# One fused cross-attention block: attention in batches of four half-width units, and a one-pass, tile-wise start

## The reference

```python
def _layernorm(x): return (x - mean(x)) / sqrt(var(x) + 1e-5)

def xattn(latents, context):          # latents = _layernorm(x)
    lat = layer_norm(latents, ln_lat_g, ln_lat_b)      # a second norm, then gain and bias
    ctx = layer_norm(context, ln_ctx_g, ln_ctx_b)
    q = heads(lat @ Wq); k, v = split(ctx @ Wkv); k = apply_rope(heads(k), cos, sin)
    attn = softmax(clip(q @ k.T * 64**-0.5, -11, 11))
    return concat(attn @ v) @ Wo + bo

x = x + tanh(g_xattn) * xattn(_layernorm(x), ctx)
x = x + tanh(g_ffn) * int8_matmul(_layernorm(x), rhs)  # both sides quantised, row and column scales
```

## Time and profile before

| What | us |
|---|---|
| median of three runs | 1541.34 |
| profiled execution, its own time | 1544.19 |
| its span (first to last instruction) | 1542.4 |
| TensorE (PE) busy | 1490.7 (97%) |
| VectorE (DVE) busy | 1287.8 (83%) |
| ScalarE (ACT) busy | 714.5 (46%) |
| GpSimd (POOL) busy | 127.8 (8%) |
| value products, L874 | 496.6 |
| score products, L861 | 426.4 |
| exps, L932 | 496.3 |
| adds, L1016 | 516.0 |
| clips, L1022 | 314.0 |

### The profile page before, as it was taken

How to read it: one execution, slowest core, us unless ns; L and a number is a source line. 1 busy time by engine, 2 the same in 40 slices (tenths; PEclk the granted TensorE clock), 3 DMA queues, 4 the chain that set the end, 5 groups by cost and what they waited for, 6 DMA issues and landing times. The chain is left out here.

```text
span 1542.4 us, 22114 instructions
## 1 busy us (share of the span) xinstructions
PE 1490.7 (97%) x7896; PEld 869.5 (56%) x7896; DVE 1287.8 (83%) x1256; ACT 714.5 (46%) x794; POOL 127.8 (8%) x72
## 2 busy tenths in 40 slices
PE   3999999999999899999999999999999999999997
PEld 3788888888886334444444444444444444444774
DVE  6866666676654999899899899899899899998887
ACT  3433222222223555555555555555555555555342
POOL 2220000000000210000000000000000000000765
PEclk9999999999999999999999999999999999999998
DMA  5665655546567540541440440441441442311652
GB/s 185 232 240 190 190 164 181 161 153 200 163 181 256 142 123 29 124 115 38 123 123 28 123 123 27 123 123 38 113 123 46 105 123 55 97 42 35 185 163 82
DMA packets 121998, 195.30 MB, mean 127 GB/s; under 512 B 18368, under 2 KB 67520, under 8 KB 115808
## 3 DMA queue, kind: packets, MB, share of 16 engines
q1 hardware_dynamic: 119360, 190.49, 42.5%
q10 hardware_dynamic: 2592, 4.20, 0.7%
HBM read 114.70 MB, written 79.95 MB: 126 GB/s over the span
## 5 line engine op out<-in xcount | busy, mean ns | idle before, releaser
L932 ACT ACTIVATE prob<-score_ps 128x1024 f32<-128x1024 f32 x512 | 496.3, 1022 | 377.7 <-PE score_ps L861 377.5
L1016 DVE TENSOR_TENSOR prob_sum<-prob_sum,prob 128x2048 f32<-128x2048 f32 x224 | 516.0, 2304 | 0.5
L874 PE MATMUL value_ps<-prob,v_st 128*64 128x512 f32 x2048 | 496.6, 606 | 10.6 <-DVE prob L1022 10.3
L861 PE MATMUL score_ps<-q_st,k_st 64*128 64x512 f32 x3072 | 426.4, 409 | 2.5 <-PEq L102 2.1
L861 PEld LDWEIGHTS score_ps<-q_st,k_st 64*128 64x128 f32 x3072 | 269.2, 185 | 256.4 <-ACT prob L932 187.8
L1022 DVE TENSOR_SCALAR prob<-prob 128x2048 f32<-128x2048 f32 x256 | 314.0, 1226 | 68.1 <-ACT prob L932 64.2
L874 PEld LDWEIGHTS value_ps<-prob,v_st 128*64 128x64 f32 x2048 | 124.2, 136 | 250.1 <-issue 201.7
L645 DVE TENSOR_TENSOR k_cos<-k_raw,rope 128x1024 f32<-128x1024 f32 x32 | 39.2, 1225 | 99.9 <-ACT k_raw L546 99.9
L551 ACT ACTIVATE v_out<-proj_ps 128x1024 f32<-128x1024 f32 x31 | 31.9, 1030 | 136.7 <-PE proj_ps L228 136.7
L546 ACT ACTIVATE k_raw<-proj_ps 128x1024 f32<-128x1024 f32 x31 | 31.9, 1029 | 105.2 <-PE proj_ps L228 104.0
L1331 POOL MEMSET unround<- 128x1 f32 x1 | 0.1, 98 | 872.6 <-POOLq L115 872.6
(11 more groups left out here) (119 smaller groups left out, 1306.2 us busy)
## 6 DMA issues: line engine op xcount, KB each, us to landing
k_st<-k_scr SPq DMA_DIRECT2D x128, 256.0 KB, 6.2
k_scr<-k_hi SPq DMA_DIRECT2D x64, 256.0 KB, 2.7
v_scr<-v_out SPq DMA_DIRECT2D x32, 512.0 KB, 3.5
k_scr<-k_lo SPq DMA_DIRECT2D x64, 256.0 KB, 4.0
q_st<-q_scr SPq DMA_DIRECT2D x16, 1024.0 KB, 10.5
v_st<-v_scr SPq DMA_DIRECT2D x16, 1024.0 KB, 13.3
q_scr<-q_hi SPq DMA_DIRECT2D x32, 256.0 KB, 3.3
q_scr<-q_lo SPq DMA_DIRECT2D x32, 256.0 KB, 3.4
```

What stands on the lines that cost most here:

```text
L861: last = pe.matmul(score_ps[:, half, a, :], k_st[slot][rows, k_part, s * P:(s + 1) * P], q_st[slot][rows, q_part, cols], start=(t == 0), s ...
L874: last = pe.matmul(value_ps[rows, cols], v_st[slot][:, s, rows], prob[:, s % PSLOT, a, cols], start=(s == 0), stop=(s == STEPS - 1))
L932: act.activation(prob[:, s % PSLOT, :, cols], score_ps[:, half, :, :], ACT.Exp, scale=SCALE).then_inc(exped, 1)
L1016: dve.tensor_tensor(total, total, prob[:, s % PSLOT, :, :], ALU.add).then_inc(added, 1)
```

## The change

It has two parts.

**Attention.** The queries of a pair are taken by halves: all 16 key steps for the first 512 queries, then for the others. A unit is one key step of one half (128x1024 with both heads), four units are a batch (BATCH_UNITS), a pair has 32 units in 8 batches, four a half. TensorE does the scores of a batch, 24 products, then the values of the batch before, 16. ScalarE makes four exps of the same size as before, VectorE one clip of 128x4096 and two adds of 128x2048 (one in the first batch of a half). Prob has two slots of one batch. The scores have three slots in PSUM, values and sums one bank each. Sums, reciprocals, the scaling and the stores are done by halves; a sum has 32 columns a head and partial sum, and VectorE joins the two partial sums in `reciprocals`. In `exps` the wait for the scores now stands last, behind those for the slot. SyncE loads pair n+2 after the reciprocals of half 0. The work on the feed-forward weight moves into pair 0 on VectorE, and the pieces of Wo to batches 1, 3, 4 and 5.

**Start.** The two norms of x become one pass with another constant under the root (eps_sq, factor 1 + eps). Chunk 0 is loaded, measured, scaled and transposed tile by tile. Wq is split by halves of its columns, and VectorE makes its rest. TensorE does 56 transposes of the identity before, and 10 behind, the transposes of chunk 0 (`keep_busy`). Tanh of the gates and its table load move behind context chunk 6.

```diff
-        def exps(n, s):
-            for half in range(2):
-                g = STEPS * n + s
-                act.wait_ge(scored, 2 * g + half + 1)
-                if not (first(n) and s < PSLOT):
-                    act.wait_ge(valued, g - PSLOT + 1)
-                    act.wait_ge(added, (STEPS - 1) * n + behind)
-                act.activation(prob[:, s % PSLOT, :, cols], score_ps[:, half, :, :], ACT.Exp, scale=SCALE)
+        def exps(n, b):
+            for u in range(b * BATCH_UNITS, (b + 1) * BATCH_UNITS):
+                if u % BATCH_UNITS == 0 and not (first(n) and b < 2):
+                    act.wait_ge(valued, BATCHES * n + b - 1)
+                    act.wait_ge(added, ADDS * (2 * n + (b - 2) // HALF_BATCHES) + 2 * ((b - 2) % HALF_BATCHES) + 1)
+                act.wait_ge(scored, UNITS * n + u + 1)
+                act.activation(prob[:, b % 2, u % BATCH_UNITS, :], score_ps[:, u % BANKS, :, :], ACT.Exp, scale=SCALE)
...
+        def scores(n, slot, b):
+            for u in range(b * BATCH_UNITS, (b + 1) * BATCH_UNITS):
+                if u >= BANKS:
+                    pe.wait_ge(exped, UNITS * n + u - BANKS + 1)
...
+        def sums(n, half):
+            for j in range(2):
+                for a in range(2):
+                    row = (2 * j + a) * SUM_ROWS
+                    last = pe.matmul(sum_ps[row:row + SUM_ROWS, :], ones[:, 0:SUM_ROWS], prob_sum[:, half, j, a, :],
+                                     start=True, stop=True)
+            for b in range(BATCHES):
+                scores(n, slot, b)
+                if b >= 1:
+                    values(n, slot, b - 1)
+                elif not first(n):
+                    values(n - 1, 1 - slot, BATCHES - 1)
+                if b == 1 and not first(n):
+                    sums(n - 1, 1)
+                if b == HALF_BATCHES + 1:
+                    sums(n, 0)
...
+            for b in range(BATCHES):
+                clip(n, b)
+                add_probs(n, b)
+                if b == 7 and not (isinstance(n, int) and n == ALLPAIRS - 1):
+                    ends.reciprocals(dve, n, 0)
+                if b == 1 and not first(n):
+                    ends.normalise(dve, n - 1, 0)
+                if b == 3 and not first(n):
+                    ends.reciprocals(dve, n - 1, 1)
+                if b == 5 and not first(n):
+                    ends.normalise(dve, n - 1, 1)
...
+        def after(n, where, before, loading=None):
+            ends.store_sums(sp, n, 0)
+            ends.load_sums(sp, n, 0)
+            if before is not None:
+                ends.store_output(sp, n - 1, 1, *before)
+            ends.store_reciprocals(sp, n, 0)
+            ends.load_reciprocals(sp, n, 0)
+            if loading is not None:
+                load(n + 2, *loading)
+            ends.store_sums(sp, n, 1)
+            ends.load_sums(sp, n, 1)
+            ends.store_output(sp, n, 0, *where)
+            ends.store_reciprocals(sp, n, 1)
+            ends.load_reciprocals(sp, n, 1)
...
+        def keep_busy(times):
+            for i in range(times):
+                pe.transpose(proj_ps[:, 3, 0:P], ident[:, :], ident[:, :])
+        pe.wait_ge(ident_set, 2)
+        keep_busy(WARM_EARLY)
+        turn_singles()
+        keep_busy(WARM_LATE)
...
+        for i, part in enumerate(SINGLE):
+            measure(0, 0, part)
+            if i:
+                normalise(0, 0, SINGLE[i - 1])
+        normalise(0, 0, SINGLE[-1])
+        wq_rest(0)
+        tok_split(0, 0)
+        wq_rest(1)
+        measure(1, 1)
```

More of the change, by code:

```diff
@@ L172, in load_reciprocals @@
+    def load_reciprocals(self, sp, n, half):
         late = self.late
-        sp.wait_ge(late.rec_stored, 16 * (n + 1))
+        sp.wait_ge(late.rec_stored[half], 16 * (n + 1))
         for a in range(2):
[L176 to L181, removed]
@@ L319, in banks, with turns_before @@
         return acc[:, first_bank:first_bank + 2, :]
-    def last_pass(n):
-        return 2 * n + 1 if isinstance(n, int) and n < QCH else n + QCH
-    def passes(n):
-        return (2 * n, 2 * n + 1) if n < QCH else (n + QCH,)
+    def turns_before(n, part):
+        return part[0].start if part is not CHUNK else n - 1
     def slot_read(eng, n):
@@ L830, in _ @@
         for n in range(2):
[L831 to L833 removed]
+            after(n, (0, n), (0, n - 1) if n else None, (n, 0, n + 2))
         with sp.Fori(1, ALLPAIRS // 2 - 1) as i:
@@ L836, in _ @@
                 n = 2 * i + slot
-                load(n + 2, slot, sp.snap((n + 2) // PAIRS), sp.snap((n + 2) % PAIRS))
-                ends.fetch_reciprocals(sp, n)
-                ends.store_output(sp, n, sp.snap(n // PAIRS), sp.snap(n % PAIRS))
-        sp.wait_ge(late.o_stored, 16 * (ALLPAIRS - 2))
+                here, last, ahead = [(sp.snap((n + d) // PAIRS), sp.snap((n + d) % PAIRS)) for d in (0, -1, 2)]
+                after(n, here, last, (slot,) + ahead)
+        n = ALLPAIRS - 2
+        after(n, (BATCH - 1, PAIRS - 2), (BATCH - 1, PAIRS - 3))
+        for half in range(2):
+            sp.wait_ge(late.o_stored[half], 16 * PAIRS)
         for t in range(2):
@@ new lines, in copy_values, with copy_sums @@
+        def copy_values(n, half):
+            act.wait_ge(valued, BATCHES * n + HALF_BATCHES * (half + 1))
+            if not first(n):
+                act.wait_ge(late.o_made, 2 * n + half - 1)
+            act.activation(late.o_raw[:, half * CH:(half + 1) * CH], value_ps[:, :], ACT.Copy).then_inc(late.o_copied, 1)
+        def copy_sums(n, half):
+            act.wait_ge(summed, 2 * n + half + 1)
+            if not (first(n) and half == 0):
+                act.wait_ge(late.sum_stored, 16 * (2 * n + half))
@@ new lines, in add_probs @@
+        def add_probs(n, b):
+            half, part = divmod(b, HALF_BATCHES)
+            total = prob_sum[:, half, :, :, :].rearrange("p j a c -> p j (a c)")
+            halves = [prob[:, b % 2, j:j + 2, :] for j in (0, 2)]
+            before = ADDS * (2 * n + half) + 2 * part - 1
+            dve.wait_ge(clipped, BATCHES * n + b + 1)
+            if part == 0:
+                if not first(n):
+                    dve.wait_ge(summed, 2 * (n - 1) + half + 1)
+                dve.tensor_tensor(total, halves[0], halves[1], ALU.add).then_inc(added, 1)
+                return
+            for j in range(2):
+                dve.wait_ge(added, before + j)
+                dve.tensor_tensor(total, total, halves[j], ALU.add).then_inc(added, 1)
@@ L1293, in turn @@
             if isinstance(t, int) and t == 3:
-                ends.reciprocals(dve, LAST)
+                for half in range(2):
+                    ends.reciprocals(dve, LAST, half)
             ending = isinstance(t, int) and t == TILES + 1
```

434 lines of the change are left out of this document (204 added, 230 removed).

## The result

Six runs of the changed kernel have a median of 1488.93 us (1487.94 to 1490.43), six of the kernel before on the same chip 1541.96 (1540.34 to 1545.64). The ratio is 0.9654, with an interval of 0.9641 to 0.9666: 53.0 us less, where 54 were predicted (1487). The profiled execution took 1488.88, its span 1486.9. That is 55.5 less span than before; the difference to 53.0 is mostly that the profiled execution of before lay 2.2 above its median and this one did not.

The account below looks back on a forecast made before the run. TensorE was taken to bound the attention, VectorE close behind. Attention 42.2 - 5.1 - 0.6 + 0.5 = 37.0 less, start and projections 17.0 less: 1490.2 from the profiled 1544.2, 1487 us against the median; range 1480 to 1507.

Parts of the forecast that it names:

- The switches: Attention: changes between score and value shapes lose 0.33 us a step; batching saves 42.2 us over 128 batches.
- Rival 4: Attention: the loss sits in each visit's waits or data, not shape, so batching saves nothing: 1529 us; chance 0.02.
- The sums: Sum products: four 32-column products at a time, 0.86 us a half plus 0.16 for a further switch, 5.1 more in all.
- rival 3: Sum products: only two run at a time, giving 1515 us; chance 0.09.
- VectorE: Attention: VectorE needs 26.4 us a half against TensorE's 27.4; clip 2.30, slack 2.4, slip up to 1.2; TensorE stays bound.
- rival 2: Attention: VectorE becomes the bound through gaps its present idling hides, 5 to 35 us more, likeliest 1500; chance 0.14.
- Pair 0: First attention pair: 61 us, with ScalarE's waits for Wo pieces passed on to TensorE; 0.6 more than now.
- The rhs work on VectorE, all in pair 0 now, uses those stalls: First attention pair: VectorE's rhs work fits into the stalls of about 1.7 + 3.3 + 3.5 + 1.3 us before exps.
- The order of the waits: ScalarE's exps: waiting for scores last spares at most two checks before each exp, keeping slack; costed at nothing.
- The last pair: End of attention: waits of 1.1 and 0.8 us, together the same as now; half-width last sum copy gives 0.5 back.
- The start: Start and projections: first product at 16.6, gain 11.3 us; clock 1.4 and chunk 2's stall 4.3; 17.0 less.
- rival 1: Start: dummy transposes don't lift the clock and push the first product to 20, giving 1492 us; chance 0.14.

Follow-up runs that it names:

- run 2: Changed kernel, but TensorE goes twice per batch from scores to values, two units each: 1566.90 us, ratio 1.0156 to the kernel before.
- run 3: Changed kernel, but exps wait for their scores first and then for the free slot: 1500.19 us, ratio 0.9728 to the kernel before.
- after: The changed kernel itself, with new attention and new start, against the kernel before: 1488.93 us, ratio 0.9654.
- run 4: Changed kernel, but sums use 64 columns a head, gathered in PSUM, without VectorE's join: 1510.85 us, ratio 0.9796 to the kernel before.
- run 8: Changed kernel with ScalarE's splits of Wo in batches 2, 4, 6, 7 of pair 0: 1490.79 us, ratio 0.9668 to the kernel before.
- run 10: Changed kernel with exps waiting for scores first in the pairs written out, last in the loop: 1486.98 us, ratio 0.9644 to the kernel before.
- run 12: Changed kernel with the edits of run 10 and run 11 and 34 dummy transposes for 10: 1483.68 us, ratio 0.9624 to the kernel before.
- run 9: Changed kernel, but GpSimd makes the rest of Wq again: 1495.28 us, ratio 0.9706 to the kernel before.
- run 11: Changed kernel with Wo's rest made by VectorE in place of GpSimd, last two pieces later: 1486.56 us, ratio 0.9644 to the kernel before.
- run 6: Changed kernel with 34 dummy transposes for 10 behind those of chunk 0: 1487.85 us, ratio 0.9647 to the kernel before.
- run 5: Changed kernel without its 66 dummy transposes: 1489.30 us, ratio 0.9659 to the kernel before.

## Why the prediction was right, point by point

**The switches.** Right in size, and shown: a round trip costs 0.35 (run 2) where I had worked out 0.33 from spacings in the earlier trace rows, and the waits inside a group cost nothing as long as they are met. Rival 4 is out. "So the shape" goes further than the runs: in run 3 the 0.11 that I had put down to entering the score shape is paid at unit 3 too, after a stop inside the group (0.33 to the next products for 0.22). A good part of the price therefore goes with a stop of the products, and no run separates shape, number format and stop for what is left.

**The sums.** Right: 1.00 a half against 1.02. Four at a time was my assumption; the starts in after and run 4, its opposite, show it, and rival 3 is out. The Trainium skill's statement on this (TensorEngine Tiling (Array Packing), Tiling Modes), that 128x32 tiles work as four independent ones, agrees with the 1.00; it gives no price for the change of mode, the 0.33 to 0.35 of the runs is one.

**VectorE.** Right in size: clips 2.286 (2.30), 95% busy, a slack over the clip of 2.1 in the batch shown and 1.0 at the least, where I had 2.4 less up to 1.2 of slipping. TensorE waits 4.3 us for clips in all, and rival 2 did not come in the steady part. Pair 0 is VectorE's, but it was so before the change: from 492.5 to 556.5 VectorE's only idle time was 12.7 us in front of clips, 9.0 of it one wait.

**Pair 0.** I predicted 61 for pair 0, and it was 60.87, but for an incomplete reason: "ACT stalls about 1.7 + 3.3 + 3.5 + 1.3 in front of exps, each passed on to TensorE". ScalarE's stalls were larger (15.5 in all), and when run 8 took them away pairs 0 and 1 together did not get shorter. The step that failed is "The rhs work on VectorE, all in pair 0 now, uses those stalls": it did not fit, and the backlog went into pair 1. Over a steady pair, pairs 0 and 1 lie 6.3 + 5.5 = 11.8, against 6.9 + 3.2 = 10.1 before: 1.7 more, where I had 0.6. Of the 1.7, 0.9 is idle time of TensorE (12.1 in the two pairs, 11.2 before) and 0.6 the later exps of pair 1, which is written out (8 x 0.08; run 10 gives 0.5 of it back). GpSimd's four pieces are part of the 11.8: where one runs, two adds take 6.67 in place of 4.62. They ran in the kernel before too, whose adds in pair 0 took 2.64 on average. That 61 was hit is luck: the cause I named was not the one that set the length.

**The order of the waits.** "I cost it at nothing" was wrong as a price. Against the batching with scores first it is worth 11.3 us: a pair of the loop takes 54.57 in place of 55.65, 13.0 in twelve pairs, and the pairs written out give 1.6 of it back. The batching has made the exps' start the tight link: that slack was 0.1 to 0.2, and the later exp used all of it. It did not harm the sum, since I took the exps' lag of 1.01 from the kernel before, and scores last gives just that (1.02). The pairs written out run at 1.09 and lose 0.08 a batch (6.65), which I had not foreseen. The mechanism is in the rows of run 3: the exp is late by 0.07 to 0.1 for each sequencer instruction that still has to run once the scores are there, none, one or two. Runs 10 and 12 bear it out, with none between and 1.00 to 1.02 in the loop and in the steady pair 14 alike. Why the compiled program places them in opposite ways in the loop and outside it stays open.

**The last pair.** The waits came as 0.71 for the clip and 1.00 for the add, where I had 1.1 and 0.8, in this chain of TensorE's timeline, answering to the earlier trace rows:

```profile
1362.08 3.65 PE L893 MATMUL value_ps<-prob,v_st 128*64 128x512 f32 x16 [0.71 <-DVE prob L1043]
1366.73 1.06 PE L907 MATMUL sum_ps<-prob_sum,ones 128*32 128x512 f32 x8 [1.00 <-DVE prob_sum L1059]
```

**The start.** First product at 16.30 (16.6), for the reason given: weights and affine on ScalarE, then the casts. Run 9 shows that taking GpSimd off VectorE's neighbourhood is 6.5 of the 11.6. The stall of chunk 2 is gone. The clock came as predicted, full for the transposes and half for 3.4 us from 16.8, behind the idle time before 16.30; run 11 shows that this fall need not come. So transposes do lift the clock, at 10.50 to 13.40 and again in run 6, where nothing but transposes ran before 16.22 and the clock was full in the next 3.8 us. The rule of the Trainium skill (TensorE: Matmul & The Clock Gate, Part 4: PE-mode transpose) says that they do not count; these runs do not agree. So rival 1 is out: 56 dummies and 16 transposes ended at 12.3 and not at 17.8. But the gain that I gave the dummies is not theirs: those of after are worth nothing (run 5), as they stop too early to spare the slow products, and what they quicken was not on the path. The 1.4 of the sum came all the same, because the slow stretch of products is about 3 us long in place of 6.2 whether they run or not (half clock from 16.8 to 20.2 in after, to 19.1 in run 5).

**Sum.** 17.5 (17.0) and 37.3 (37.0). That the attention is hit so closely is luck, errors that cancel: steady pairs 0.19 shorter than I had (3.0 in 16 pairs), against 1.1 more than I had in pairs 0 and 1, 0.6 in pair 14, and 0.8 in the last pair (0.3 lost over a steady pair, where I had 0.5 back).

## What to carry to other kernels

Where products of two tile shapes alternate on TensorE, read the spacing inside a group and at its edges: the difference is the price of a visit, and batching is worth it only as far as the consumers' buffers (here the third score slot) and the checks in front of the next engine's instruction leave slack. Once a change has used up such a slack, the order of waits, costed at nothing before, has a price per batch. When a stall vanishes in one stretch and turns up in the next, as in run 8, the engine that was busy through both is the bound, whatever the stalls are named after.

## What the runs showed of the hardware

- The order of two waits that are both met or almost met moves an exp by 0.14 us (1.02 to 1.16 behind its scores) in the loop, and the other way by 0.07 in pairs written out. It goes with the sequencer instructions left between: 0.07 to 0.1 each, at 0.035 to 0.038 of their own.
- A stop of 0.07 inside a group of score products is followed by a spacing of 0.33 in place of 0.22 to 0.23 (run 3, unit 3).
- GpSimd beside VectorE: two casts took 8.68 in place of 1.29, beside 9.41 of a subtraction on GpSimd; two adds 6.67 in place of 4.62 beside 3.86 of one.
- Eight plain float32 products of 32 columns take 1.00 with the change of shape, of 64 columns 1.71.
- The granted clock was full behind 128x128 float32 transposes alone. It fell to half for 3.4 us after 2.9 us of idling in after, for 6.8 in run 10 with the same start, and not at all in run 11 after 2.35 us.
- In every kernel the clock also fell once or twice during the first two pairs, where TensorE has idle time (in after at 515.1 for 3.4 us, in the kernel before at 546.1 for 3.4).
